# Moving the transposition of each head's row of largest scores one step later in the order of TensorE and VectorE

## What is computed

```
attn = jax.nn.softmax(attn, axis=-1)                  # layer 0, all keys
scores = jnp.where(causal, scores, -jnp.inf)          # layer 1, keys up to the query
attn = jax.nn.softmax(scores, axis=-1)
out = jnp.einsum('bhqk,bhkd->bhqd', attn, v)
```

## Time and profile before

| what | value |
|---|---|
| median of 3 runs | 3036.42 us (3030.33 to 3038.16) |
| profiled execution, its own time | 3037.59 us |
| its span in the trace | 3035.9 us |
| mean granted clock of TensorE | 0.957 of full |
| PE busy | 2700.3 us (89%) |
| DVE busy | 2223.7 us (73%) |
| POOL busy | 1781.9 us (59%) |
| ACT busy | 1767.0 us (58%) |

### The profile page before, as it was taken

One profiled execution on the slowest core, in us unless ns is written; L12 is line 12 of the kernel. 1 busy time (PEld: TensorE's weight loads), 2 busy tenths in 40 slices (PEclk: granted clock), 3 DMA queues, 4 the chain that ended last, 5 costly groups with the idle time before them and its releaser, 6 DMA issues.

```text
span 3035.9 us, 68416 instructions
## 1 busy us (share of the span) xinstructions
PE 2700.3 (89%) x29020; PEld 1576.3 (52%) x29020; DVE 2223.7 (73%) x3769; ACT 1767.0 (58%) x2091; POOL 1781.9 (59%) x1181
## 2 busy tenths in 40 slices
PE   5899888999889988899989999899988999889995
PEld 3455544556446563465635655355553655535562
DVE  6786868767777777867777687686876868767684
ACT  5565645646556566564565655656555565555563
POOL 5374764737547375583756746466464665647464
PEclk8999999999999999999999999899999999999998
DMA  3000001000100001000010000100001000010000
GB/s 118 22 2 1 2 22 43 2 1 2 43 22 2 1 2 43 22 2 1 2 43 22 2 1 2 54 11 2 1 2 63 2 2 1 2 43 2 2 2 22
DMA packets 32751, 48.11 MB, mean 16 GB/s; under 512 B 5152, under 2 KB 32032, under 8 KB 32448
## 3 DMA queue, kind: packets, MB, share of 16 engines
q1 hardware_dynamic: 30944, 43.13, 4.3%
q10 hardware_dynamic: 1504, 0.61, 0.1%
HBM read 30.95 MB, written 12.58 MB: 14 GB/s over the span
## 4 chain that ended last, share of the span: by engine, by line
PE 42%; DVE 21%; POOL 16%; issue 13%; ACT 7%; DMA 0%; POOLq 0%; DVEq 0%; SPq 0%; ACTq 0%
PE ps L547 10%; POOL pl L995 8%; PE ps L881 6%; POOL ph L1038 5%; DVE mxp L951 5%; PE ps L671 4%; PE ps L842 4%; PE ps L851 4%; PE ps L806 4%; DVE pl L995 3%; ACT qa L655 2%; DVE stats L1115 2%; PE ps L844 2%; DVE x L1111 2%; PE ps L1090 2%
## 5 line engine op out<-in xcount | busy, mean ns | idle before, releaser
L995 POOL TENSOR_TENSOR pl<-p,ph 128x1024 f16<-128x1024 f32 x336 | 822.7, 2448 | 406.0 <-ACT ph L928 381.6
L951 DVE TENSOR_REDUCE mxp<-ps 128x1 f32<-128x512 f32 (+2 forms) x1344 | 777.4, 626 | 180.0 <-PE ps L806 172.2
L926 ACT ACTIVATE p<-ps 128x1024 f32<-128x1024 f32 (+1 forms) x672 | 644.1, 960 | 450.4 <-PE ps L851 444.1
L881 PEld LDWEIGHTS ps<-v,ph 128*128 128x128 f16 x9600 | 517.7, 98 | 133.0 <-issue 42.6
L995 DVE TENSOR_TENSOR pl<-p,ph 128x1024 f16<-128x1024 f32 (+1 forms) x336 | 426.5, 1269 | 214.4 <-POOL ph L1038 209.2
L881 PE MATMUL ps<-v,ph 128*128 128x65 f16 (+1 forms) x9600 | 541.9, 195 | 22.7 <-DVE pl L995 14.9
L881 PE MATMUL ps<-v,pl 128*128 128x65 f16 x4800 | 519.3, 194 | 0.0
L881 PEld LDWEIGHTS ps<-v,pl 128*128 128x128 f16 x4800 | 452.8, 100 | 0.0
L851 PE MATMUL ps<-qc,kc 65*128 65x512 f16 (+3 forms) x1344 | 388.5, 371 | 0.0
L686 POOL TENSOR_TENSOR v<-o,v 128x384 f16<-128x384 f32 x128 | 113.2, 889 | 444.6 <-ACT o L682 444.6
L928 ACT ACTIVATE ph<-p 128x1024 f16<-128x1024 f32 x336 | 355.2, 1057 | 10.7
(11 more groups left out here) (189 smaller groups left out, 5244.7 us busy)
## 6 DMA issues: line engine op xcount, KB each, us to landing
xin<-in_x SPq DMA_DIRECT2D x8, 1536.0 KB, 7.0
x<-in_x SPq DMA_DIRECT2D x8, 1536.0 KB, 8.0
out<-x SPq DMA_DIRECT2D x16, 768.0 KB, 3.6
qc<-rowt SPq DMA_DIRECT2D x96, 2.0 KB
o<-in_L_conv_qkv_w SPq DMA_DIRECT2D x2, 576.0 KB, 10.3
p<-in_L_conv_qkv_w SPq DMA_DIRECT2D x1, 576.0 KB, 11.4
x<-in_L_attn_Wq SPq DMA_DIRECT2D x1, 576.0 KB, 12.1
x<-in_L_attn_Wk SPq DMA_DIRECT2D x1, 576.0 KB, 13.0
```

The lines of the kernel that those rows point to most:

```text
L881: mm = nc.tensor.matmul(m.ps[:, 6 + half % 2, c0:c0 + w], e, v, start=(first and n == 0), stop=(g in self.last_of_half and n == len(work) ...
L926: nc.scalar.activation(m.p32[:, i % RING, :, 0:w], m.ps[:, 2 * (i % 2):2 * (i % 2) + 2, 0:w], ACT.Exp, scale=SCALE).then_inc(s["exp"], 1)
L951: nc.vector.reduce_max(m.mxp[:, h % 2, kh, qt:qt + 1], m.ps[:, bank, 0:w], AX.X).then_inc(s["free"], 1)
L995: engine.tensor_tensor(m.pl[:, i % RING, :, 0:w], m.p32[:, i % RING, :, 0:w], m.ph[:, i % RING, :, 0:w], ALU.subtract).then_inc(sem, 1)
```

## The change

One number changes in the table: the row of heads 1 to 5 is entered one step later, in both layers. The max pieces, `nm`, and the step in which the row is needed stay.

```diff
@@ -729,7 +729,7 @@
             if end > begin:
                 for n in range(self.NTL):
                     steps[begin + n * (end - begin) // self.NTL].append(("max", h, n))
-            steps[end].append(("row", h))
+            steps[end + 1].append(("row", h))
         for c in range(NC_ - 1):
             for hf in range(2):
                 steps[(2 * c + 2) * G + LAG + 1 + hf].append(("ot", c, hf))
```

## The result

The changed kernel took 3085.7 us median against 3033.05 us for the kernel before; the ratio is 1.0166, with a 95% interval of 1.0143 to 1.0189. It is slower by some 50 us, where 6 us faster was forecast, and it lies above the range. Two of the six executions of the changed kernel (3228.0 and 5890.8 us) were disturbed by the chip: they count in this median and in no ratio, and the other four have a median of 3083.4 us. The profiled execution has a span of 3085.5 us. The kernels of each group of runs were timed beside the kernel before on the same chip.

What follows compares the result with a forecast made beforehand. PE's idle time and lower clock were taken as the bound. Layer 0 -46 us, layer 1 +38 and clock +2 gave -6 us, 3030.4 against a median of 3036.4, stated as 3031; range for 8 in 10: 3014 to 3051.

Steps and rivals of the forecast that it cites:

- What bounds the kernel: PE, 89% busy, loses time idling and at the lower clock; the moved transpositions at L811 meet at most 41 us idle.
- Layer 0, head 1: L851 of step 8 comes at 1251.1, not 1253.55: gain 2.4 us in each of 8 images, 19 us.
- Head 5: Layer 0: L851 of step 40 comes at 1345.3, not 1348.58: gain 3.3 us in each of 7 images, 23 us.
- Head 4: Layer 0: frees 1.01 us, but 0.7 us returns at step 31's second max piece: gain 0.3 us in 7 images.
- Layer 1, heads 1 to 4: Late rows cost 1.9 us at head 2, 1.7 at head 4, 0.3 at head 3, nothing at head 1, per image.
- Layer 1, head 5: Row lands at 1489.7 against 1487.47, 2.2 us late; 0.9 us an image stays after a later wait absorbs some.
- That wait is eaten: Layer 1, head 5: PE's 1.56 us wait at 1493.21 for a low half slow beside POOL absorbs part of the 2.2 us delay.
- Clock: New stalls are split, so the lower clock follows few of them: +2 us, between 0 and +27 us.
- Slower: layer 1's stalls bring the lower clock: Rival: stalls at heads 2 and 4 cost up to 1.7 us more each: 3065 us, or 3047 for half; chance 0.13.
- The time for the DMA (1.7 us): From the end of the row's copy to its landing, taken between 1.4 us to the last data and 3.2 us.
- The value of 2.0 us: The skill page's fixed DMA cost in place of 1.7 us: some +8 us in all, making the sum +2 us.

Runs made afterwards that it cites:

- copy_first: As the changed kernel, but DVE copies the row ahead of the low half of the same step: 3002.5 us, ratio 0.9906.
- heads15_hold_pool: Against the kernel before: layer 0 rows of heads 1 and 5 moved, copied first; layer 1 POOL low halves of steps 4, 30 held for DVE's: 3000.96 us.

## Why the prediction was wrong, step by step

**What bounds the kernel: right.** The stalls at L811 went, and new ones came at the lines that were named, with L824 at head 5 the longest. From its first to its last L881 layer 0's attention is 5.0 us shorter in images 0 to 6, where about 6 was forecast, and layer 1's is 9 us longer, not 5.

**Layer 0, head 1: right.** 2.4 us forecast, 2.4 us measured. **Head 5:** 3.3 us forecast, 2.7 us measured at the same place. **Head 4: wrong sign.** I let the second max piece of step 31 wait 0.7 us for the row's bank; the view of waits has 14.8 us for 15 such waits, 7 of them here at 1.2 us and 8 at head 3 of layer 1; 1.2 us is more than the 1.01 us that the move saved there. Together with a last image that gave less, layer 0 is -33 us where I had -46.

**Layer 1, heads 1 to 4: right.** 3.9 us an image forecast, 3.7 us measured by the runs without head 5; heads 2 and 4 to 0.1 us. The stall at the bank came as forecast (1.5 us); the short one behind it at L851 did not show, since the rows landed just in time.

**Layer 1, head 5: this is the step that failed.** The prediction put "low half 1486.62 to 1487.8, copy to 1488.0" and then "0.9 us stays". It took the 1.23 us of the low half from the earlier trace rows for a property of the instruction. It is the length that it has when DVE starts first. The row for it was at hand: `nm`, a tiny instruction, took 2.06 us in the earlier trace rows, where it started 0.09 us behind a low half of POOL, and POOL's low half took 3.06 us at this very place. With L811 gone from step 27, POOL no longer waits for ACT ahead of its low half, overtakes DVE by 0.07 us, and the low half on DVE ends 1.9 us later; the stall at L824 is 3.3 us and not 1.5 (1488.0 less 1486.46, in the prediction's times), the lower clock follows it, and the second meeting delays the last products. Measured by taking it out: 53 us, not 7. That it is who starts first is shown by the runs that hold POOL back, which return 28 and then 9 us more of the 53; what is left is about 2 us an image by the attentions' lengths, near the 0.9 us of the forecast. That L811 is what flipped the order is argued: from L851 of step 27 to L851 of step 28 PE took 1.88 us before and takes 1.63 us without it, and ACT's high half is so much earlier. The copy can be ruled out, as copy_first shows, but no run moves L811 alone.

**"That wait is eaten", the 1.56 us at 1493.21: right at that place, wrong in what it leaves.** No such wait stands in the step where it was. But the second meeting, at 1516.02, makes a new one in every image, and the waits of L881 for DVE's low half are 18.3 us in all, where they were 14.9 us:

```profile
1519.31 0.22 PE L881 MATMUL ps<-v,ph 128*128 128x65 f16 x2 [1.34 <-DVE pl L995]
```

```profile
PE ps L881 <- DVE pl L995: 18.3, 20, 1.3
```

**Clock: right for heads 2 and 4, too small in all.** I expected stalls that leave it alone, and those of heads 2 and 4 do; but the one long stall of head 5 was followed by the lower clock in all 8 images. Holding POOL back saved 28 us where the stall alone is 8 x 1.9 = 15 us. In the traces 5 us of the rest lie in layer 1's attentions, where the lower clock behind the stall is gone in 6 of 8 images, and the other part lies behind the last attention. There the changed kernel's profiled execution is 8 us longer than that of the kernel before, with 8 us more of PE busy at a lower mean clock. From the last L881 to the end, changed kernel, then before:

```profile
3018.70:3085.50 66.80, 38.69 (x163) 12.80 (x159) 23.95 (x58) 17.11 (x19) 17.16 (x14) 0.59 0.07 24
```

```profile
2977.20:3035.90 58.70, 30.18 (x159) 11.48 (x155) 23.96 (x58) 17.01 (x19) 17.14 (x14) 0.76 0.08 27
```

Nothing of the change is in that stretch, so up to 8 of the 50 us may be no cost of the change. The kernel that holds POOL once has 57.8 us there and the one that holds it twice 66.6 us. Why the lower clock stays there in some executions is open.

**The rivals.** "Slower: layer 1's stalls bring the lower clock" had the right sign and, at 3065, half of the size, but named heads 2 and 4, and it was head 5. The time for the DMA (1.7 us) held: at head 5 the copy ends at 1503.99, and L851, which the landing released, starts at 1505.76, 1.77 us later. The value of 2.0 us fits worse; the section of the Trainium skill that it comes from ("DMA: Bandwidth & Descriptors", Anatomy of one DMA) is on DMAs that GpSimd issues, and the row's is issued by SP. By the prediction's own terms it would have added 9 us, not 8.

## What to carry to other kernels

A transfer is covered from the moment at which its source is written, not from the moment at which the work is listed: moving the transposition by a step moved the copy behind a low half and cost in layer 1 over two times what layer 0 saved. When an order changes, look at every pair of instructions on DVE and POOL that start within a few tenths of a microsecond of each other, and price both orders; the length in the trace belongs to one of them. Ask what releases each: here one event released both, and whether POOL had still to wait for ACT decided the order. And where a table serves two layers with steps of 2.5 us and of 1.6 us, try the change in each alone: layer 0 alone is 1.1% faster, the whole 1.7% slower.

## What the runs showed of the hardware

Two subtractions with two operands in SBUF each, one on DVE (1.23 us alone) and one on POOL (2.13 us alone), do not run side by side. Whoever starts second takes its own time and nearly all that the first still needs: 3.13 us on DVE when POOL started 0.07 us ahead, 3.06 us on POOL when DVE started 0.16 us ahead. A start of a tenth of a microsecond thus decides which of two engines loses 1 to 2 us. A small instruction is hit as well: `nm` took 0.17 us with POOL idle and 2.06 us behind POOL's low half, here in the kernel before, DVE and then the POOL row beside the 2.06 us of the earlier trace rows:

```profile
1482.81 0.17 DVE L988 TENSOR_SCALAR nm<-mxp 128x8 f16<-128x8 f32 x1
```

```profile
1337.61 2.12 POOL L995 TENSOR_TENSOR pl<-p,ph 128x1024 f16<-128x1024 f32 x1
```

The Trainium skill has this rule in "SBUF — State Buffer", SBUF: two separate sides: the port pair that DVE and GpSimd share is "an exclusive lock, not a bandwidth split", and the one that starts first keeps it for its whole instruction. The trace agrees within 0.15 us: 2.12 us of POOL less the 0.07 us of head start and 1.23 us make 3.28 us, against 3.13 us measured. I had not used it in the prediction.

An added wait can be worth 28 us if it restores the better order, and it can also be worth nothing or less, as in heads15_hold_pool, where it only moved the wrong order to the next two steps.
